# One chain of the scan at a time, and another order of the beginning, in a fused Mamba and attention kernel on one core

## The reference, cut to what matters

```python
# x: (128, 64, 256); cond: (128, 512). Layer 0, per sequence of 64 tokens:
xr, gate = split(x @ W_in.T, 2)                 # 512 channels each
xr = xr + cond[:, None, :]
xc = silu(causal_conv_4_taps(xr) + b_conv)
xn = layernorm(xc) * ln_g + ln_b
Bm, Cm, dt = split(xn @ W_xproj.T, 3)           # 16 states each
dt = tanh(dt @ W_dt.T + b_dt) * 0.01
Ad = 1 - dt * tanh(A_log)
Bd = Bm * minimum(norm(xn), 1)
h = clip(h * Ad[t] + Bd[t] * xn[t], -10, 10)    # for t in 0..63, h is 16 x 512
y[t] = Cm[t] @ h
x = x + (y + D * xn) * silu(gate) @ W_out.T
# Layer 1, per sequence: s1, s2 = cond[:, :256], cond[:, 256:]
z = layernorm(x * s1)
dc_w = rsqrt(square(w) @ square(s) + 1e-8)      # for q, k, v, w, u
attention over 16 heads of 16, keys, values and output scaled by dc, plus a skip
```

## Time and profile before

| what | us |
| --- | --- |
| median of 3 executions | 1804.61 (1801.22 to 1805.07) |
| the profiled execution's own time | 1796.04 |
| its span, first to last instruction | 1794.1 |
| before the first scan update | 164.4 |
| steps 8 to 19 of the list | 228.0 |
| steps 20 to 66 (all full) | 1097.1 |
| steps 67 to the end | 304.6 |

### The profile page before, as it was taken

How to read it: one execution, slowest core, us unless ns; L and a number is a source line. 1 busy time by engine, 2 the same in 40 slices (tenths; PEclk the granted TensorE clock), 3 DMA queues, 4 the chain that set the end, 5 groups by cost and what they waited for, 6 DMA issues and landing times. The chain is left out here.

```text
span 1794.1 us, 41468 instructions
## 1 busy us (share of the span) xinstructions
PE 1610.8 (90%) x12460; PEld 1042.8 (58%) x12460; DVE 1341.5 (75%) x2306; ACT 1160.8 (65%) x2921; POOL 1226.3 (68%) x1874
## 2 busy tenths in 40 slices
PE   5345877799999999999999999999999999999886
PEld 4233333356666666666666666666666655555664
DVE  1423577788888888888888888888888888876442
ACT  3555554567777777777777777777777753444453
POOL 1587766787888887878787887888787873233231
PEclk8657777999999999999999999999999999999998
DMA  4013445565566556565655565556666564533220
GB/s 106 16 54 69 107 105 127 140 147 147 147 148 148 142 131 171 130 167 136 156 147 145 142 149 147 146 144 155 146 149 148 132 163 113 132 89 92 77 66 24
DMA packets 222716, 224.27 MB, mean 125 GB/s; under 512 B 54241, under 2 KB 179553, under 8 KB 222497
## 3 DMA queue, kind: packets, MB, share of 16 engines
q1 hardware_dynamic: 222496, 221.62, 50.8%
HBM read 150.36 MB, written 71.17 MB: 123 GB/s over the span
## 5 line engine op out<-in xcount | busy, mean ns | idle before, releaser
L1635 DVE CUSTOM_DVE_ANT_0 gc<-ps_u,gc,hi 128x512 f32<-128x512 f32 x1008 | 776.4, 803 | 56.3 <-PE ps_u L948 37.3
L964 PE MATMUL ps_y<-gc,cms 128*32 128x512 f32 x2048 | 301.5, 622 | 9.0 <-POOL cms L660 7.2
L1256 ACT ACTIVATE a_tap<-a_xr,conv_w 128x128 f32<-128x128 f32 x768 | 245.0, 399 | 14.8 <-DVE a_xr L1567 9.5
L948 PE MATMUL ps_u<-xs_sb,stage 64*128 64x512 bf16 x1024 | 201.3, 433 | 29.4 <-issue 18.4
L538 POOL TENSOR_TENSOR a_tap<-a_tap 128x512 f32<-128x512 f32 x128 | 163.1, 1278 | 65.2 <-ACT a_tap L1256 65.0
L902 PE MATMUL ps<-a_xT,WinT 128*128 128x128 f32 x1024 | 143.4, 300 | 20.6 <-ACT a_bcT L1304 14.7
L902 PEld LDWEIGHTS ps<-a_xT,WinT 128*128 128x128 f32 x1024 | 135.8, 214 | 36.4 <-issue 29.3
L948 PEld LDWEIGHTS ps_u<-xs_sb,stage 64*128 64x128 bf16 x1024 | 75.2, 187 | 103.6 <-issue 70.5
L993 PE MATMUL ps<-WinT,c_xT 128*128 128x512 f32 x256 | 127.3, 620 | 3.7 <-ACT c_xT L1327 3.7
L1031 PEld LDWEIGHTS ps<-c_zT,L1T 128*128 128x128 f32 x1024 | 123.8, 192 | 7.4 <-issue 4.3
L1031 PE MATMUL ps<-c_zT,L1T 128*128 128x128 f32 x1024 | 125.1, 275 | 3.1 <-ACT c_kbd L1377 3.1
(11 more groups left out here) (168 smaller groups left out, 3651.6 us busy)
## 6 DMA issues: line engine op xcount, KB each, us to landing
xs_sb<-xn_parts SPq DMA_DIRECT2D x256, 192.0 KB
xn_parts<-a_parts SPq DMA_DIRECT2D x128, 192.0 KB, 3.0
skip_d_xn<-a_dx SPq DMA_DIRECT2D x64, 256.0 KB, 2.0
xs_sb<-xn_parts SPq DMA_DIRECT2D x128, 128.0 KB
scan_out<-y_sb SPq DMA_DIRECT2D x256, 64.0 KB
c_dx<-skip_d_xn SPq DMA_DIRECT2D x64, 256.0 KB, 3.5
c_y<-scan_out SPq DMA_DIRECT2D x64, 256.0 KB, 3.2
c_wu<-style_rows SPq DMA_DIRECT2D x128, 128.0 KB, 3.4
```

What stands on the lines that cost most here:

```text
L948: pe.matmul(ps_u[r][t % 2][:, :], weights[:, :, l * STEPS + t], xs_sb[rows, l % 2, t, :], start=True, stop=True).then_inc(s[f"b_u{r}"], 1)
L964: pe.matmul(ps_y[quad:quad + 32, :], cms[:, slice_no(*chain_of(sig, r)) % 2, v, r, 32 * u:32 * (u + 1)], gc[r][:, (2 * u + v) % RING, :], ...
L1256: ins = act.activation(a_tap[:, tap, m, :].rearrange("p (r t) -> p r t", r=2), a_xr[:, m, :, tap:tap + S], ACT.Identity, bias=bias, scale= ...
L1635: dve._custom_dve(bass.dve_ops.TENSOR_ADD_SAT, out=gc[r][:, t % RING, :], in0=ps_u[r][t % 2][:, :], in1=before, s0=hi[:, c % 4, col:col + ...
```

## The change

The change has four parts.

1. The scan works on one chain at a time. The two halves r now hold the even and the odd time steps of the same chain, so a step of the list covers 16 time steps of one chain (`SPAN`), and a chain takes 4 steps. `scan_step` for r reads the `gc` that the update just before it wrote. `load_w` writes the weights of a chain into both halves.
2. C_LAG is 13, so stage C starts four steps earlier and the list has 81 steps. first: 0 to 6; second: 7 to 12; full: 13 to 66; late: 67 to 72; last: 73 to 80.
3. The beginning: W_in and cond are loaded first, PE transposes five groups and the small projection, then does step 0; the projections' norm fold and the other seven groups stand behind step 0. The inverse roots are done for one weight at a time behind steps 2 to 6, in other tiles than `stage`; `stage` is cleared in four pieces behind steps 2 to 5. In `first_step` DVE does `a_half`, `a_sum`, `a_gain` and `a_shift`, five instructions that POOL did.
4. The order inside `first_step`, `second_step`, `step` and `late_step` is another on every engine; `last_step` is unchanged.

```diff
-    SLICES = S // STEPS
+    SPAN = 2 * STEPS
+    SLICES = S // SPAN
...
-    C_LAG = 17
+    C_LAG = 13
     A_DEPTH = 3
+    ROOT_STEPS = 6
+    CLEAR_STEP = 2
     STEP_COUNT = TILES + C_LAG + 4
-    SCAN_STEPS = TPC * CHAINS + TPC
+    SCAN_STEPS = TPC * CHAINS
...
-    def chain_of(sig, r):
-
-        g = sig - TPC * r
-        c = 2 * (g // SLICES) + r
-        return (c, g % SLICES) if g >= 0 and c < CHAINS else None
+    def chain_of(sig):
+
+        return divmod(sig, SLICES) if 0 <= sig < SCAN_STEPS else None
...
-        dco = stage[:, 6144:7424].rearrange("p (w o) -> p w o", w=5)
-        dm_x = stage[:, 3072:4352]
-        dm_t = stage[:, 4352:5632]
+        dm_x = five(c_kbd[:, :, :, :].rearrange("p h k t -> p (h k t)"), c_f2)
+        dm_t = five(c_x1[:, :, :].rearrange("p w o -> p (w o)"), c_xm)
+        dco = five(c_e[:, :, :].rearrange("p g t -> p (g t)"), c_z)
...
             def load_w(c):
-
-                r = c % 2
                 sp.wait_ge(s["b_bst"], 48 * (c + 1))
...
                 for k in range(SEQS):
-                    sp.dma_start(Wb[r * ROWS + k:(r + 1) * ROWS:SEQS, c // 2 % 2, k, :],
-                                 bdt_dram[c, :, k * DS:(k + 1) * DS, :].rearrange("e d t -> e (d t)"))\
+                    sp.dma_start(Wb[k:2 * ROWS:SEQS, c % 2, k, :],
+                                 bdt_dram[c, :, k * DS:(k + 1) * DS, :].rearrange("e d t -> e (d t)").unsqueeze(0)
+                                 .to_broadcast([2, TERMS, DS * S]))\
                         .then_inc(s[f"b_ld_w{c % 4}"], 16)
...
+                    pe.wait_ge(s[f"b_g{r}"], HEAD + q - 1)
+                    rows = slice(r * ROWS, (r + 1) * ROWS)
+                    weights = Wb[rows, c % 2, :, :].rearrange("p k (d t) -> p (k d) t", d=DS)
+                    pe.matmul(ps_u[r][t % 2][:, :], weights[:, :, l * SPAN + 2 * t + r], xs_sb[rows, sig % 2, t, :],
+                              start=True, stop=True).then_inc(s[f"b_u{r}"], 1)
...
+                if i == 0:
+                    fold_norm()
+                    transpose_rest()
                 if i == 1:
                     sum_squares()
...
+            def invert_root(w):
+
+                done = 5 * w
+                dve.wait_ge(s["w_de"], 6 + w)
+                dve.reciprocal(dco[w], dco[w]).then_inc(s["w_dm"], 1)
+                dve.wait_ge(s["w_dm"], done + 1)
+                dve.tensor_tensor(dm_t[w], dco[w], dco[w], ALU.mult).then_inc(s["w_dm"], 1)
+                dve.wait_ge(s["w_dm"], done + 2)
+                dve.tensor_tensor(dm_t[w], dm_t[w], dm_x[w], ALU.mult).then_inc(s["w_dm"], 1)
+                dve.wait_ge(s["w_dm"], done + 3)
+                dve.tensor_scalar(dm_t[w], dm_t[w], -0.5, 1.5, ALU.mult, ALU.add).then_inc(s["w_dm"], 1)
+                dve.wait_ge(s["w_dm"], done + 4)
+                dve.tensor_tensor(dco[w], dco[w], dm_t[w], ALU.mult).then_inc(s["w_dm"], 1)
...
-                dve.wait_ge(s[f"b_g{r}"], HEAD + q)
+                dve.wait_ge(s[f"b_g{1 - r}"], HEAD + q + r)
                 dve.wait_ge(s[f"b_read{r}"], 8 * HEAD + 2 * ((q - RING) // 2 + 1))
-                before = zeros[:, :] if col == 0 else gc[r][:, (t - 1) % RING, :]
+                before = zeros[:, :] if col == 0 else gc[1 - r][:, (t - 1 + r) % RING, :]
```

More of the change, by code:

```diff
@@ L220, in mamba_attention_kernel, with five @@
         st_dt = c_th[0:DS, :]
+        def five(wide, last):
+            return [wide[:, w * DM:(w + 1) * DM] for w in range(4)] + [last[:, :]]
+        dm_x = five(c_kbd[:, :, :, :].rearrange("p h k t -> p (h k t)"), c_f2)
+        dm_t = five(c_x1[:, :, :].rearrange("p w o -> p (w o)"), c_xm)
+        dco = five(c_e[:, :, :].rearrange("p g t -> p (g t)"), c_z)
         g_wide, b_wide = c_sg, c_yg
@@ L281, in mamba_attention_kernel @@
                                WinT[:, k, h * 512:(h + 1) * 512]))
+        groups.append(([(m * P, cond_nat[:, m * P:(m + 1) * P]) for m in range(MC)],
+                       condT[:, :, :].rearrange("p m b -> p (m b)")))
         for mp in range(2):
@@ L288, in mamba_attention_kernel @@
                            L1T[:, w, :, :].rearrange("p k o -> p (k o)")))
-        groups.append(([(m * P, cond_nat[:, m * P:(m + 1) * P]) for m in range(MC)],
-                       condT[:, :, :].rearrange("p m b -> p (m b)")))
         NG = len(groups)
-        W_LOADS = 5 + 3
-        W_CONSTS = 11 + SEQS
+        FIRST_GROUPS = 2 * KC + 1
+        W_LOADS = 1 + 5
+        W_PROJ = 5
+        W_CONV = 2
+        W_CONSTS = 4 + SEQS
         W_POOL = 7
@@ L951, in read_out @@
             def read_out(sig, u):
-                live = [r for r in range(2) if chain_of(sig, r)]
-                for r in live:
-                    c, l = chain_of(sig, r)
+                if not chain_of(sig):
+                    return
+                for r in range(2):
                     if u == 0:
-                        pe.wait_ge(s[f"b_cms{r}"], HEAD + slice_no(c, l) + 1)
-                    pe.wait_ge(s[f"b_g{r}"], HEAD + slice_no(c, l) * STEPS + 2 * u + 2)
-                if u == 0 and live:
+                        pe.wait_ge(s[f"b_cms{r}"], HEAD + sig + 1)
+                    pe.wait_ge(s[f"b_g{r}"], HEAD + sig * STEPS + 2 * u + 2)
@@ L1208, in _ @@
             give_head_start(act, "act")
-            for g, (_, dst) in enumerate(groups):
+            for g, (_, dst) in enumerate(groups[:FIRST_GROUPS]):
                 act.wait_ge(s["w_tp"], g + 1)
                 act.activation(dst, bank[g % 2][:, :], ACT.Copy).then_inc(s["w_ev"], 1)
-            act.wait_ge(s["w_tp"], NG + 1)
-            act.activation(WxT[:, :, 0:2 * DS],
-                           bank[0][:, 0:MC * NPROJ].rearrange("p (m k) -> p m k", m=MC)[:, :, 0:2 * DS],
-                           ACT.Copy).then_inc(s["w_ev"], 1)
@@ new lines, in take_rest @@
+            def take_rest():
+                for g, (_, dst) in enumerate(groups[FIRST_GROUPS:]):
+                    act.wait_ge(s["w_tp"], FIRST_GROUPS + 1 + g + 1)
+                    act.activation(dst, ps_u[1][g % 2][:, :], ACT.Copy).then_inc(s["w_ev"], 1)
+                act.wait_ge(s["w_ev"], NG + 4)
+                act.activation(stage[:, 0:2560], L1T[:, :, :, :].rearrange("p w k o -> p (w k o)"), ACT.Square)\
+                    .then_inc(s["w_sq"], 1)
+                act.activation(stage[:, 2560:3072], condT[:, :, :].rearrange("p m b -> p (m b)"), ACT.Square)\
+                    .then_inc(s["w_sq"], 1)
+                act.wait_ge(s["w_cst"], W_CONSTS * 16)
+                act.activation(a_col[:, 1:2], a_col[:, 0:1], ACT.Tanh).then_inc(s["w_a"], 1)
```

715 lines of the change are left out of this document (376 added, 339 removed).

## The result

The changed kernel is slower by 0.8%: 1817.4 us (median of 7 runs, 1810.3 to 1823.6) against 1801.2 for the kernel before on the same chip, a ratio of 1.0081 with a 95% interval of 1.0057 to 1.0106. The forecast was 1730, with a range of 1697 to 1772. The profiled execution took 1813.5, with a span of 1811.8.

The account below looks back on a forecast made before the run. The prediction took PE to bound the full steps at 23.3 us each. Its terms, -29 - 69 + 104 - 80 = -74, put the span of 1794.1 at 1720 and the median at 1730, range 1697 to 1772.

Parts of the forecast that it names:

- Term 1: Beginning: tile 0 starts sooner and early steps take 13.4 us; first update at 135, -29 us.
- Rival 3: Early steps: contention of DVE and POOL takes most of the gain, -13 in place of -29, 1746; chance 0.11.
- term 3: Full steps 16 to 66: 51 where 47 stood, plain ones still 23.2, preparing ones 1.5 longer; +104 us.
- Term 2: Steps 8 to 15 replace steps 8 to 19: 159 us where 228 stood, -69 us.
- The wait for `c_yg`: Preparing steps: PE waits 0 to 1.6 us for what it transposes, taken as 1.3 a chain.
- Term 4: End: four half-filled late steps go, the six that stay are as long as before; -80 us.
- Rival 1: Full steps: DVE becomes the bound, each takes 0.5 to 0.8 us more, 1765 in all; chance 0.18.
- Rival 4: Full steps: update chain and PE's blocks end up in series, 26.6 us a step, 1914; chance 0.05.
- Rival 2: Preparing steps' new waits don't show and the beginning goes faster: -18 and -12, 1700; chance 0.16.

Follow-up runs that it names:

- run 6: Changed kernel with DVE's full step reordered, statistics and divide first, `c_silu` last: ratio 1.0000 to the kernel before.
- run 4: Changed kernel without the weight loads of chains 2 to 15 and PE's wait for them (result differs): ratio 0.9860 to the kernel before.
- run 7: Changed kernel with each update reading the same r's result one step back (result differs): ratio 0.9914 to the kernel before.
- run 1: Changed kernel with prepared B stored twice, so each weight load reads 16 equal rows: 1795.0 us, ratio 0.9961 to the kernel before.
- run 11: Changed kernel with doubled B store, statistics and divide first, `c_silu` last, prepare two updates sooner, B's store ahead of x loads: 1757.5 us, 0.9747.

## Why the prediction was wrong, step by step

**Term 1, the beginning: the sum is right, in part by luck.** The first update came at 136.6 (133.0 to 141.7 over the traces of all its runs), forecast 135; the early steps stood 13.6 apart, (104.81 - 50.53) / 4, forecast 13.4. Rival 3 is out. But step 2's copy of the transposed x came at 45.6 where "about 50" was forecast, and the stretch from `prepare` to the first update, "16.0, which I leave as it is", took 22.1:

```profile
45.58 0.36 ACT L1276 ACTIVATE a_xT<-ps 128x256 f32<-128x256 f32 x1
114.48 0.24 DVE L1686 TENSOR_SCALAR ad<-raw,a_col 128x64 f32<-128x64 f32 x1
136.62 0.81 DVE L1704 CUSTOM_DVE_ANT_0 gc<-ps_u,zeros,hi 128x512 f32<-128x512 f32 x1 [7.39 <-PE ps_u L970]
```

The two errors cancel nearly. Of the 6.1 us in the second, 3.4 lie between the weights' last issue and the update (5.7 for 2.3), so the late loads of term 3 were at work here already.

**Term 2: right in its kind, short by 10.** Steps 8 to 10 took 17.14 for 17.2. Step 11 took 29.2 for 23: the raw load landed later than I had it (prepare at 194.2, not 192.8), four stores of y in place of two held the store of B (4.4 us behind the split's end, before 1.8), and the loads took longer to land. The 18.2 from prepare to first update were 23.0 here. I had taken them over whole from a step with half the stores and loads of half the rows.

**Term 3 is where the forecast failed**, by 65 of the 92 us, in two sentences. First, "a plain full step stays at 23.2, hidden by 1.2 us of DVE's slack". DVE had even more slack than that, its 22.0 were 20.8, but slack over a whole step doesn't hide anything that PE waits for in the middle of one. I checked DVE's sum and not the moment at which it gives back each bank that PE asks for next. PE waits 0.57 a step for bank 2, which `c_divide` empties late, and run 6 took just this away by order alone; another 0.17 goes to the bank that `a_xr` empties. So a plain step took 23.93, and the 0.73 above 23.2 are 37 in 51 steps. Second, the weights "an unknown from 0 to 1 us a chain": they cost 2.2 of wait a chain, up to 3.5, and 0.7 more at a chain's first step, which at the lower clock takes 24.7 in place of run 4's 23.9. By run 4 the full steps have 25 us of it (1241.3 against 1215.8). The unknown was named and its upper bound was too low, because only the rows were counted and not on how many DMA engines the new form puts them (1.4 us from last issue to last landing became 4.4); and because the clock's answer to a wait had no term at all. Together these are 62, where the sum held 12 x 0.2 = 2 for them. The wait for `c_yg` was right: 1.07 a chain for 1.3. So 57 of the 65 us have a name, and 8 don't.

**Term 4: the saving is there, and 15 us less than forecast**: step 67 took 30.8 and step 68 22.1, where 20.3 was meant, and run 4 gives back 8.8 of these 12. Most of what is left is one more wait for `c_o`, 2.6 in step 67 with and without the reload:

```profile
1575.58 0.66 PE L1122 MATMUL ps<-ident,c_o 128*128 128x128 f32 x2 [2.64 <-DVE c_o L1788]
```

Steps 69 and 70 took 20.9 and 20.8, a little more than forecast too.

**The rivals.** Rival 1 had the size of a plain step's loss, 0.5 to 0.8, at 0.18, and half of its mechanism: the dependent updates do make PE wait (run 7), but at the bank that `c_divide` empties and not at the scan blocks, and its reason, a full DVE, is wrong. That it came together with late weights was in no case. Rival 4 (1914) is out: it alone lay on the slower side, where the outcome is, but it would show as PE waiting for `gc`, and in steps 16 to 65 PE never does. Rival 2 is the reverse of what happened.

**What stays open**: why PE still waits for `a_xr` 0.17 in three of four steps wasn't followed up, and neither was why SP's queue holds the store of step 67 so long (in run 1 it left 6.8 us behind the split, 1562.84 against 1556.0). The gain of run 11 over run 1 isn't divided among its edits.

## What to carry to other kernels

An engine with slack in the sum can still be late at one place: for each bank or buffer that the bounding engine takes, find the instruction that empties it and what stands ahead of it in its queue. A chain of queue issues, a landing and a wait has to be costed by where the issue stands in SP's queue and by how the form of the transfer spreads over engines, not by bytes; and when such a chain sets the end of a step, time saved elsewhere in that step only lengthens the wait, so cut the chain first and then the rest. Where a forecast rests on a slack near zero, its range should hold the case that the slack isn't there.

## What was not expected of the hardware

- A repeated dimension in a load's source changed the last landing of a chain from 1.4 us behind the last issue to 4.4 (3.4 to 5.3), at much the same issue time of 0.5 to 0.6 each; with 16 equal rows it was 1.6, and in the old form with twice as many loads 1.4.
- PE's granted clock over the step behind a chain's first block, at 132 such places (steps 20 to 60 of the changed kernel and its eleven edited forms): of the 28 with no wait or one under 1.0 us, 27 kept 1.00; of the 45 with more than 2.5, 43 had 0.90 to 0.96, in a step longer by 1 to 3 us, and among these are all 24 with 3 or more; between, both occur. The wait of 3.5 us shown above cost 5.2 with the 1.7 that PE then worked longer.
- The doubled store of B took 0.9 us more up to its landing (6.9 for 6.0 on average), though it writes twice the bytes.
